# First attention layer of a two-layer transformer: GpSimd work placed after the row shifts, value products in four beats, expert weights loaded from ScalarE's queue, output projection first in its beat

## The reference

```python
h = layernorm(x) * (1 + ca) + sa
x = x + ga * attention0(h)       # 16 heads of 8, causal mask, softmax
h = layernorm(x) * (1 + cb) + sb
x = x + gb * moe(h)              # 8 routed experts, 2 chosen, and a shared one
h = layernorm(x) * (1 + ca1) + sa1
x = x + ga1 * attention1(h)      # 16 heads of 8, ALiBi bias, no mask
h = layernorm(x) * (1 + cb1) + sb1
x = x + gb1 * spikes(h)          # squared relu, 5 spiking steps
```

## Time and profile before

| what | value |
|---|---|
| median of three runs | 1060.96 us |
| the profiled execution's own time | 1063.57 us |
| its span | 1061.8 us |
| mean granted TensorE clock | 0.972 |
| PE busy | 947.9 us (89%) |
| VectorE busy | 783.9 us (74%) |
| ScalarE busy | 753.1 us (71%) |
| GpSimd busy | 536.7 us (51%) |

### The profile page before, as it was taken

How to read it: one execution, slowest core, us unless ns; L and a number is a source line. 1 busy time by engine, 2 the same in 40 slices (tenths; PEclk the granted TensorE clock), 3 DMA queues, 4 the chain that set the end, 5 groups by cost and what they waited for, 6 DMA issues and landing times. The chain is left out here.

```text
span 1061.8 us, 23047 instructions
## 1 busy us (share of the span) xinstructions
PE 947.9 (89%) x8688; PEld 519.1 (49%) x8688; DVE 783.9 (74%) x1324; ACT 753.1 (71%) x1380; POOL 536.7 (51%) x748
## 2 busy tenths in 40 slices
PE   5788789889898999999999989999999999899896
PEld 3333334333344888888877733333333333333564
DVE  4777767778792676766677768888898888895465
ACT  2477677778776666566555469888888888888663
POOL 3465655675553022213210148785867778666344
PEclk8699999999999999999999989999999999999999
DMA  6323412211202733333322110212112020200011
GB/s 177 110 82 87 136 51 86 79 50 41 84 15 55 186 93 101 90 91 109 111 83 87 52 52 30 75 32 64 31 54 73 14 74 26 70 11 16 23 31 50
DMA packets 63582, 73.91 MB, mean 70 GB/s; under 512 B 14120, under 2 KB 45992, under 8 KB 63088
## 3 DMA queue, kind: packets, MB, share of 16 engines
q1 hardware_dynamic: 62608, 71.66, 23.4%
q10 hardware_dynamic: 864, 0.79, 0.4%
HBM read 39.24 MB, written 2.77 MB: 40 GB/s over the span
## 5 line engine op out<-in xcount | busy, mean ns | idle before, releaser
L862 ACT ACTIVATE at_E<-at_Sb 128x512 f32<-128x512 f32 x832 | 445.6, 599 | 81.2 <-PE at_Sb L715 75.7
L926 DVE TENSOR_REDUCE mx<-at_Mb 128x2 f32<-128x1024 f32 x242 | 281.9, 1217 | 43.0 <-PE at_Mb L678 41.8
L763 PE MATMUL at_Ob<-at_E,VP 128*32 128x256 f32 (+2 forms) x2816 | 213.9, 377 | 16.6 <-ACT Oev L890 10.4
L715 PE MATMUL at_Sb<-QP,KP 64*128 64x512 bf16 (+3 forms) x1024 | 204.5, 347 | 10.4 <-ACT full_k L417 3.6
L1028 POOL TENSOR_TENSOR at_E<-at_E,factor 128x512 f32<-128x512 f32 x128 | 162.4, 1273 | 76.8 <-ACT at_E L862 66.8
L678 PE MATMUL at_Mb<-KP,QP 62*128 62x512 bf16 x996 | 174.5, 356 | 18.0 <-DVE mx L926 15.4
L929 DVE TENSOR_REDUCE mx<-at_Mb 128x2 f32<-128x768 f32 (+1 forms) x128 | 138.4, 1087 | 57.0 <-PE at_Mb L678 55.7
L1039 POOL TENSOR_SCALAR_AFFINE_SELECT at_E<-at_E 128x512 f32<-128x512 f32 x128 | 82.7, 659 | 76.4 <-ACT at_E L862 76.4
L763 PEld LDWEIGHTS at_Ob<-at_E,VP 128*32 128x32 f32 x2816 | 57.1, 108 | 119.7 <-issue 88.1
L715 PEld LDWEIGHTS at_Sb<-QP,KP 64*128 64x128 bf16 x1024 | 74.9, 96 | 72.3 <-ACT at_E L862 36.1
L1468 DVE TENSOR_TENSOR ex_hh<-ex_R,ex_th 128x512 f32<-128x512 f32 x88 | 64.5, 733 | 60.1 <-ACT ex_th L1406 59.4
(11 more groups left out here) (207 smaller groups left out, 1446.2 us busy)
## 6 DMA issues: line engine op xcount, KB each, us to landing
QP<-q SPq DMA_DIRECT2D x96, 128.0 KB, 2.4
KP<-k SPq DMA_DIRECT2D x90, 128.0 KB, 2.4
ex_R<-rw_dram SPq DMA_DIRECT2D x32, 256.0 KB, 3.9
ctxN<-Oev SPq DMA_DIRECT2D x16, 256.0 KB, 3.0
denB<-rdram SPq DMA_DIRECT2D x64, 64.0 KB
ex_R<-rw_dram SPq DMA_DIRECT2D x16, 224.0 KB, 4.1
ex_R<-rw_dram SPq DMA_DIRECT2D x16, 192.0 KB, 3.6
ex_R<-rw_dram SPq DMA_DIRECT2D x16, 160.0 KB, 3.5
```

What stands on the lines that cost most here:

```text
L715: return pe.matmul(out[:, at:at + SEQ - q0], KP[p0:p0 + ROWS_H, b % 2, 2 * g + a, kt * P:(kt + 1) * P], QP[p0:p0 + ROWS_H, b % 2, 2 * g + ...
L763: last = pe.matmul(Ob[VW * i:VW * (i + 1), 0, q0:q1], weights_of(b, G, kt, i, q0), moving, start=(kt == 0 and q0 == 0), stop=False, skip_g ...
L862: nc.scalar.activation(dst, src, ACT.Exp).then_inc(s["s_read"], 1)
L926: v.tensor_reduce(mx[:, G % 2, :, t % 2, t // 2], src, AX.X, ALU.max).then_inc(s["m_read"], 1)
```

## The change

Five edits, all but the last confined to the first attention layer:

- the last piece of the values (key tile 2) moves from beat 9 of a group to beat 8, so `values` uses the beats 5 to 8; `read_O`, tied to the last of them, moves from beat 9 to beat 8 too, and the phase has one beat less;
- the q split moves from beat 18 to 19 of a batch, behind the shifts;
- `finish_weights` moves from beat 22 of its batch to beat 2 of the next, behind shifts and diagonal unit;
- the three expert-weight DMAs leave SyncE's queue and are issued by ScalarE at beat 12 of batches 1, 2 and 3;
- `out_proj` moves from the end of its beat to right behind `max_score`, in both layers.

```diff
-        CHUNKS = ({5: ((0, 0, 256),), 6: ((0, 256, 512),), 7: ((1, 128, 512),), 8: ((3, 384, 512),), 9: ((2, 256, 512),)}
+        WEIGHTS_AT = BPB + 2 if causal else OUT_AT + 3
+
+        CHUNKS = ({5: ((0, 0, 256),), 6: ((0, 256, 512),), 7: ((1, 128, 512),), 8: ((3, 384, 512), (2, 256, 512))}
                   if causal else
...
             for beat in range(START, END):
                 if m_of(beat) is not None:
                     max_score(*m_of(beat))
+                if out_of(beat) is not None:
+                    out_proj(out_of(beat))
                 for _, G, t, c in slots_S(beat):
                     key_score(G, t, c)
...
-                if out_of(beat) is not None:
-                    out_proj(out_of(beat))
...
                 if off == 0 and 0 <= G < ALLG:
                     read_O(G)
+                if causal and beat % BPB == 12 and 1 <= beat // BPB <= 3:
+                    w, src = ((sb["w_raw"]["w1"], "w1"), (sb["w_raw"]["w3"], "w3"), (sb["w2"], "w2"))[beat // BPB - 1]
+                    a.dma_start(w[:], dram[src]).then_inc(sb["experts_loaded"], 16)
...
-                if at == Q_AT + 1 and FIRST <= n + 2 <= last_b:
+                if at == Q_AT + (2 if causal else 1) and FIRST <= n + 2 <= last_b:
                     split("q", n + 2)
...
-                if at == OUT_AT + 3 and 0 <= n <= last_b:
-                    if n == 0:
+                if at == WEIGHTS_AT % BPB and 0 <= n - WEIGHTS_AT // BPB <= last_b:
+                    if n == WEIGHTS_AT // BPB:
                         p.wait_ge(sb["gates_ready" if causal else "gates_late"], 16)
-                    finish_weights(p, sb, s, layer, n)
+                    finish_weights(p, sb, s, layer, n - WEIGHTS_AT // BPB)
...
-                if 1 <= b <= 3 and causal:
-                    dst, src = ((sb["w_raw"]["w1"], "w1"), (sb["w_raw"]["w3"], "w3"), (sb["w2"], "w2"))[b - 1]
-                    sp.dma_start(dst[:], dram[src]).then_inc(sb["experts_loaded"], 16)
```

## The result

| | before | after |
|---|---|---|
| median of 20 runs each, us | 1064.2 (1058.0 to 1069.3) | 1070.91 (1066.4 to 1077.1) |
| ratio, 95% interval | | 1.0071 (1.0056 to 1.0087) |
| profiled execution, its own time and span, us | 1063.57, 1061.8 | 1074.54, 1072.8 |
| granted clock | 0.972 | 0.967 |
| experts' first product / second attention from, to, us | 335.3 / 620.3, 985.1 | 327.9 / 613.0, 996.2 |

A forecast was written before the change was run, and what follows sets the result against it. PE was taken to pace both attentions. First attention -14 us (30.9 less 7.9 and 9), second +7.2 for the projection's wait and +2.4 for the clock: -4.4, so 1056.6 us by the median, range 1046 to 1067.

The forecast's parts named there:

- I take two falls in the five batches: 2 x 1.2 = +2.4, bounds 0 and 6: Second attention: idle time before the projection drops PE to 1.2 GHz twice in five batches, +2.4 us.
- Rival 3: Clock drops behind the late gather in six batches and the head wait in five: 1067.3 us, slower; chance 0.17.
- The wait at the head: Second layer's projection waits 1.34 us for VectorE's reduction; five batches x 1.25 and part of two more, +7.2 us.
- Rival 2: Projection at the head costs nothing, because VectorE makes the time good: 1047 us; chance 0.13.
- First attention, what goes: Waits for shifts 12.3, evictions 10.4, phase end 1.1 and six 1.2 GHz stretches 7.1 us go: 30.9 us together.
- First attention, what is late next: Two chains do not get shorter and take back 7.9 and 9 us, leaving 14 us less in the first attention.
- the k split: First attention: values wait 1.78 us behind GpSimd's split and masks where 0.46 stood, in six batches, +7.9 us.
- the gather: First attention: the earlier eviction waits for `ctxN`, ScalarE about 1.8 us in batches 1 to 6; PE loses 9 us.
- The signature: Signs expected in the profile after, among them ScalarE's `ctxN` wait three to six times longer in all.
- both chains: First attention: GpSimd's k split and masks ahead of the values, +7.9 us, and the `ctxN` gather ahead of `read_O`, +9.
- Rival 1: First attention: the chains have unseen slack, the gather lands before the eviction is due: 1047.5 us; chance 0.15.
- The expert weights: First attention: issuing these loads from ScalarE at beat 12 costs 0, at most 1.9 us; new time helps, new queue doesn't.

The follow-up runs named there:

- head only: The kernel before with one edit, the output projection at the head of its beat (behind `max_score`) in both layers: 1079.5 us, ratio 1.0153.
- the values in five beats: The changed kernel with the first layer's values back in five beats as before, all else still changed: 1059.5 us, ratio 0.9952.
- The last group: The changed kernel with VectorE's layernorm statistics and their aggregation one beat earlier in the second layer: 1061.3 us, ratio 1.0001; the same in the fastest kernel: 1042.8 us.
- the fillers: The kernel before, projection at the head in both layers, unused key products ahead of it in the second layer: five 1074.1 us, ten 1086.7 us.
- the next beat: The changed kernel with the second layer's projection one beat later, at the head of beat 23 instead of 22: 1064.6 us, ratio 0.9996.

## Why the prediction was wrong

It was to be 4.4 us less for the profiled execution, and was 11.0 more. Of the 15.4 us between, 8.8 lie in the second attention and 6.6 in the first. By the medians, +6.7 was measured where -4.4 was forecast. The 2.6 us that I took off for the median of three runs were no offset either: over 20 runs that median is 1064.2, above the profiled execution.

- **The step that failed: "I take two falls in the five batches: 2 x 1.2 = +2.4, bounds 0 and 6".** There were four stretches at 1.2 GHz, two of double length, 20 us in all where one of 3.4 stood before. They cost 5.1 us of slower matmuls. Both number and size were wrong. A batch with one stretch was 1.5 us longer, one with a stretch and the long wait 3.1, and those with a double stretch and the long wait 4.4. I had the sum of idle time in front of me (0.53 + 1.34) and set it above the 1.70 that led to falls in the first layer, and yet took two out of five; in head only, after and the values in five beats together 13 of the 15 full waits had a fall next to them. The last group bears the cause out: the same wait, its neighbours smaller and farther off, and no fall in that trace.
- **A term that the sum did not have**: PE's waits for VectorE ahead of the maxima grew by 5.9 us (15.4 to 21.3). Three times 1.1 are VectorE's blocked instruction. About 2.3 more are pairs of waits (0.6 to 1.0, then 0.52) that PE has just behind VectorE's late `den`: three pairs in the same three batches, one such before. Neither is the price of the head. In before no instruction was blocked, in ten other kernels with the projection at the end of its beat in the second layer one to three were.
- **Rival 3** was nearest in time and not in place: it had falls behind the late gather in six batches and at the head in five, and there were one (271.7) and four.
- **The wait at the head** was exact: six waits, 7.8 us, and 1.30 a batch, for 7.2 and 1.25. Rival 2 fell with it. That VectorE sets it is shown by the fillers (wait filled, batch no shorter) and by the next beat (0.74).
- **First attention, what goes**: shifts and evictions went in full (12.3 and 10.4), and the clock gave 5.1 of 7.1, for two reasons that partly cancel. The six stretches were dearer than 6 x 1.2: against the kernel with the values in five beats, which has none, they cost PE 10.7 us (256.98 to 246.31), and my 1.2 compared 30 matmuls with 39 of another mix. But they did not all go: after has four, worth 5.6.
- **First attention, what is late next**: the k split cost 7.6 (the mask 8.8 for 4.7, `full_k` 3.5) for 7.9 forecast, and at one place 1.21 + 0.59 = 1.80 us for 1.78; the gather 10.3 (`nrow` 5.5, shift rows 4.8) for 9. The signature was only half right: ScalarE's `ctxN` waits did not grow in all (5.5 for 5.6), though PE's loss behind them did. "Three to six times longer" did not follow from my own sum either, where 6 x 1.8 = 10.8 us is about twice. Not in my sum were 2.2 us more for VectorE's maxima and 1.3 for the projection; and the last batch, which was to gain 1.1, took 31.6 us for 28.4.
- **What I did not add up: the edits one by one.** The values in four beats bring the 10.4 of the evictions and cause both chains, -10.4 + 7.9 + 9 = +6.5 us. By my own terms this edit was a loss; I summed the phase and not the edit. The experiments give it 11.4 us with the clock, so that the others in the first layer are worth about 19 us of span (335.3 to 316.1). Rival 1 (slack in the chains) fell with it: the gather held up ScalarE in five batches.
- **The expert weights**: their new time helps and their new queue costs nothing that shows, as forecast.
- The Trainium skill (TensorE: Matmul & The Clock Gate, What's actually happening) has the activity judged in windows that run free of the kernel. The trace agrees: the same row of waits (1.56, 0.53 and 1.37 or 1.38 us) stands beside 6.8 us at 1.2 GHz from 742.7 and beside 3.4 from 892.9.

What stays open: why a row of the shorter waits (0.48, 0.52 and 1.34) gives a double stretch in some batches of other kernels and none at 842.84, and why the gather of `den` is late in some batches.

## What to carry to other kernels

Price each edit of a bundle by itself, with the chains that it makes late, before summing the phase: here one of five edits took back 11.4 of the 19 us of the others, and without it and the second layer's head the bundle is a gain of 1.5%. An instruction moved ahead of its neighbours paid its wait in full, and as the engine had stood idle shortly before, the clock raised the bill, up to double (head only: 15.7 us, with 7.7 of waits at the projection); look at the waits of the few microseconds ahead of the new place, not at the new wait alone. Filling a wait with dummy work gave back a third here (5.4 of 15.7 us) and did harm when there was more of it than wait: idle time ahead of it stays.

## What the runs showed of the hardware

A VectorE tensor_scalar of 128x4 that begins while a GpSimd tensor_tensor of 128x512 runs ends only with it: 1.26 us for 0.17, three times of six in the kernel after. In all 24 such cases of the twenty traces GpSimd had begun 25 to 36 ns ahead; with the instruction 1 us into the product it was 0.30. The Trainium skill (SBUF — State Buffer, Who interferes with whom) says that the two share one pair of ports under an exclusive lock and that tensor_scalar can take it, while reductions never contend; the trace agrees, for the reductions beside the same products kept their 1.21 us. What I had not expected is that some 130 ns in the order of two engines decide over 1.1 us, and often over the clock behind it.
